# Where the first attention vectors of a four-layer graph network are folded: behind the first expert layer, or between the tiles of an edge count

## What is computed

```python
h = (x @ W.T).reshape(n, heads, out_ch)          # 8 heads of 128
a_src = jnp.einsum('nhc,hc->nh', h, att_src)
a_dst = jnp.einsum('nhc,hc->nh', h, att_dst)
e = leaky_relu(a_src[src] + a_dst[dst], 0.2)     # per edge, then softmax over dst
```

## Time and profile before

| what | value |
|---|---|
| median of 3 runs | 1740.7 us (1740.62 to 1742.16) |
| profiled execution, first to last instruction | 1740.0 us (the page gives no time of its own outside the span) |
| PE busy | 1682.7 us, 97% of the span |
| DVE, POOL, ACT busy | 931.1, 690.3, 466.8 us |
| mean granted TensorE clock | 0.988 |
| mean DMA rate | 57 GB/s |

### The profile page before, as it was taken

How to read it: one execution, slowest core, us unless ns; L and a number is a source line. 1 busy time by engine, 2 the same in 40 slices (tenths; PEclk the granted TensorE clock), 3 DMA queues, 4 the chain that set the end, 5 groups by cost and what they waited for, 6 DMA issues and landing times.

```text
span 1740.0 us, 25810 instructions
## 1 busy us (share of the span) xinstructions
PE 1682.7 (97%) x10227; PEld 1579.9 (91%) x10227; DVE 931.1 (54%) x1879; ACT 466.8 (27%) x875; POOL 690.3 (40%) x428
## 2 busy tenths in 40 slices
PE   8799999999999988899999999999999999999999
PEld 7699999997999988799377888989999999998999
DVE  8993537416866679857497554423112141225731
ACT  6443123203223138934222211101011011112310
POOL 1026865652445520060020175431644435342663
PEclk9899999999999999899899999999999999999999
DMA  2002222423212210014010022111221111110222
GB/s 90 1 28 70 73 69 65 142 78 128 64 55 64 64 56 10 1 47 143 7 43 1 11 85 64 57 45 37 73 64 55 46 51 59 55 55 30 64 73 72
DMA packets 42000, 99.84 MB, mean 57 GB/s; under 512 B 10509, under 2 KB 12143, under 8 KB 41895
## 3 DMA queue, kind: packets, MB, share of 16 engines
q1 hardware_dynamic: 37828, 87.87, 16.3%
q10 hardware_dynamic: 4066, 10.46, 1.7%
HBM read 96.39 MB, written 1.92 MB: 57 GB/s over the span
## 4 chain that ended last, share of the span: by engine, by line
PE 82%; DVE 11%; ACT 4%; issue 1%; POOL 1%; DVEq 0%; POOLq 0%; ACTq 0%
PE bank L2421 10%; PE bank L2423 10%; PE bank L2422 10%; PE banks L2421 9%; PE banks L2422 9%; PE banks L2423 9%; PE bank L2983 3%; PE banks L2983 3%; PE bank L3060 3%; PE bank L3065 3%; PE banks L3060 2%; PE banks L3065 2%; DVE tmp L1827 1%; DVE src_hot L1491 1%; PE banks L2835 1%
## 5 line engine op out<-in xcount | busy, mean ns | idle before, releaser
L833 POOL TENSOR_TENSOR w_hi<-raw,ones_r 128x768 fp32r<-128x768 f32 (+1 forms) x192 | 294.0, 1532 | 994.9 <-PE banks L2423 368.3
L836 POOL TENSOR_TENSOR w_lo<-raw,w_hi 128x768 fp32r<-128x768 f32 (+1 forms) x192 | 370.5, 1930 | 15.0
L2421 PE MATMUL bank<-w_hi,xT_hi 128*125 128x384 f32 (+2 forms) x560 | 187.8, 335 | 1.7 <-DVE small L1968 1.2
L2423 PE MATMUL bank<-w_hi,xT_lo 128*125 128x384 f32 (+2 forms) x560 | 186.7, 333 | 0.0
L2422 PE MATMUL bank<-w_lo,xT_hi 128*125 128x384 f32 (+2 forms) x560 | 186.5, 333 | 0.0
L2421 PE MATMUL banks<-w_hi,xT_hi 128*125 128x384 f32 (+2 forms) x440 | 151.8, 345 | 0.2 <-DVE xT_lo L1569 0.2
L2422 PE MATMUL banks<-w_lo,xT_hi 128*125 128x384 f32 (+2 forms) x440 | 151.4, 344 | 0.0
L2423 PE MATMUL banks<-w_hi,xT_lo 128*125 128x384 f32 (+2 forms) x440 | 151.3, 344 | 0.0
L1618 DVE TENSOR_TENSOR hT_lo<-tmp,hT_hi 128x312 fp32r<-128x312 f32 (+1 forms) x88 | 94.3, 1078 | 41.9 <-ACT hT_hi L970 41.5
L2421 PEld LDWEIGHTS bank<-w_hi,xT_hi 128*125 128x125 f32 x560 | 103.9, 186 | 5.0 <-DVE small L1968 1.4
L2422 PEld LDWEIGHTS bank<-w_lo,xT_hi 128*125 128x125 f32 x560 | 103.9, 185 | 2.5
(11 more groups left out here) (579 smaller groups left out, 3923.4 us busy)
## 6 DMA issues: line engine op xcount, KB each, us to landing
raw<-wa SPq DMA_DIRECT2D x92, 384.0 KB, 3.0
raw<-wc SPq DMA_DIRECT2D x76, 384.0 KB, 3.0
raw<-wb SPq DMA_DIRECT2D x28, 448.0 KB, 3.3
w_rows<-w_in ACTq DMA_DIRECT2D x1, 3072.0 KB, 12.6
bias<-bias_in ACTq DMA_DIRECT2D x6, 384.0 KB
w_first<-w_in ACTq DMA_DIRECT2D x1, 2304.0 KB, 11.2
w_down<-w_down_in SPq DMA_DIRECT2D x8, 288.0 KB, 5.2
w_up<-w_up_in SPq DMA_DIRECT2D x1, 2304.0 KB, 10.6
```

The source lines that it names most:

```text
L833: pool.tensor_tensor(w_hi[:, k, 0:width], raw[:, k, 0:width], ones[:, 0:1].to_broadcast([P, width]), ALU.mult).then_inc(S("unit_high"), 1)
L836: pool.tensor_tensor(w_lo[:, k, 0:width], raw[:, k, 0:width], f(w_hi[:, k, 0:width]), ALU.subtract).then_inc(S("unit_split"), 1)
L2421: tell_used(pe.matmul(dst, l_hi, r_hi, start=start, stop=False))
L2423: return pe.matmul(dst, l_lo, r_hi, start=False, stop=stop)
```

## The change

The fold moves to the front of the kernel, into span 1 of the edge count.

- **Transfers.** SP, not ACT, issues them, behind the first three units of weights. Seven heads go to `w1_first`, which lies where `w_hi` and `w_lo` will be, one to `w1_last`. POOL waits for the second `g2_fold` group before its first split.
- **PE.** `count_edges` gets a function `beside`. For span 1 the loop is written out, and behind each tile from 4 on `beside(t)` is called. Behind tile 6 it waits for the transfers; behind each of the tiles 6 to 21 it issues one of the 16 matmuls; behind tile 25 it issues the six transposes.
- **ACT.** Behind its `xn` tiles and ahead of the counts of span 1 it copies the two groups to `fold_T` and the turned ones to a new `fold_full`; behind the counts of span 1 it writes `folded_1` from that.
- **DVE.** The remainder is taken at the same place as before, from `fold_full`.
- **Banks.** The three groups get banks 2, 3 and 4 between spans 0 and 1, and the rotation ahead of f1 is put back to what it was.

```diff
-    def sweep(label, before_last=()):
+    def sweep(label, in_second=(), before_last=()):
         for i in range(SPANS * NT):
-            if i == LASTS:
-                for group in before_last:
-                    add(*group)
+            for group in in_second if i == NT else before_last if i == LASTS else ():
+                add(*group)
             add(label, i, label + "_settled", i + 1)
...
-    several("g2_fold", 2, "g2_fold_copied")
     several("g1a_agg", 2 * KD, "g1a_low")
-    several("g2_foldT", 1, "g2_fold_read")
...
             for k in range(RING):
                 sp.dma_start(raw[:, k, 0:UNIT], wa[k]).then_inc(S(f"raw_full{k}"), 16)
+            sp.dma_start(w1_first[:], w1_in[0:HEADS - 1].rearrange("h p k -> p h k")).then_inc(S("w1_loaded"), 16)
+            sp.dma_start(w1_last[:], w1_in[HEADS - 1]).then_inc(S("w1_loaded"), 16)
+            sp.dma_start(att_1[:], heads_in.rearrange("p h t e -> p h (t e)")).then_inc(S("w1_loaded"), 16)
...
+            await_group(pool, "g2_fold", 1)
             pool.wait_ge(*E("A_fraction", LASTS))
...
+            for c in range(2):
+                await_group(act, "g2_fold", c)
+                act.activation(fold_T[:, c * 384:(c + 1) * 384], bank("g2_fold", c)[0:16, 0:384], ACT.Copy
+                               ).then_inc(S("g2_fold_copied"), 1)
+            await_group(act, "g2_foldT", 0)
+            act.activation(fold_full[:], bank("g2_foldT", 0)[:, 0:16 * KD].rearrange("p (k c) -> p k c", c=16), ACT.Copy
+                           ).then_inc(S("g2_fold_taken"), 1)
             counts("A", adj, 1)
+            act.wait_ge(*E("g2_fold_taken", 1))
+            act.activation(folded_1[:, :, 0:16], fold_full[:], ACT.Copy).then_inc(S("g2_fold_high"), 1)
...
-            TT(folded_1[:, :, 32:48], bank("g2_foldT", 0)[:, 0:16 * KD].rearrange("p (k c) -> p k c", c=16),
-               f(folded_1[:, :, 0:16]), ALU.subtract).then_inc(S("g2_fold_read"), 1)
+            TT(folded_1[:, :, 32:48], fold_full[:], f(folded_1[:, :, 0:16]), ALU.subtract).then_inc(S("g2_fold_read"), 1)
...
                     for t in range(OSLOTS):
                         step(span, t, t, first=t == 0)
+                    if span == 1 and beside:
+                        for t in range(OSLOTS, tiles):
+                            step(span, t, t % OSLOTS, last_tile=t == tiles - 1)
+                            beside(t)
+                        continue
...
+            def fold_attention(t):
+
+                i = t - FOLD_FIRST
+                if i == 0:
+                    pe.wait_ge(*E("w1_loaded", 48))
+                if 0 <= i < 2 * HEADS:
+                    c, h = divmod(i, HEADS)
+                    dst = open_bank("g2_fold", c) if h == 0 else bank("g2_fold", c)
+                    weights = w1_first[:, h] if h < HEADS - 1 else w1_last[:]
+                    last = pe.matmul(dst[0:16, 0:384], att_1[:, h], weights[:, c * 384:(c + 1) * 384], start=h == 0,
+                                     stop=h == HEADS - 1)
+                    if h == HEADS - 1:
+                        close(last, "g2_fold", c)
+                if t == FOLD_TURN:
+                    pe.wait_ge(*E("g2_fold_copied", 2))
+                    pe.wait_ge(*E("consts", CONSTS))
+                    dst = open_bank("g2_foldT", 0)
+                    for k in range(KD):
+                        last = pe.transpose(dst[:, 16 * k:16 * k + 16], fold_T[:, k * P:(k + 1) * P], ident[0:16, 0:16])
+                    close(last, "g2_foldT", 0)
+
+            count_edges("A", greatest, fold_attention)
```

More of the change, by code:

```diff
@@ L86 @@
 ROWS_AT = {1: 0, 2: 1}
+FOLD_FIRST, FOLD_TURN = 6, 25
 SOURCES_AT = {3: (0, 1), 5: (2,), 7: (3,), 8: (4,), 10: (5,), 11: (6,), 13: (7,)}
@@ L273, in pairs @@
             add(label, i, label + "_read", i + 1)
-    sweep("A", (("g0_maxT", 0, "g0_max_read", 1), ("g0_maxB", 0, "g0_maxB_read", 1)))
+    sweep("A", (("g2_fold", 0, "g2_fold_copied", 1, False, 2), ("g2_fold", 1, "g2_fold_copied", 2, False, 3),
+                ("g2_foldT", 0, "g2_fold_taken", 1, False, 4)),
+          (("g0_maxT", 0, "g0_max_read", 1), ("g0_maxB", 0, "g0_maxB_read", 1)))
     spare = [1, 2, 7, 0, 3, 4, 5, 6]
@@ L296, in plan_groups @@
     turned_behind("g1b", "g1_x", "f1", between=lambda: several("g2_maskT", 2 * NT, "g2_masked"))
+    spare = spare[3:] + spare[:3]
     ffn("f1", 8)
@@ L454, in families @@
     base = 0
-    for event, n in (("g2_fold_copied", 2), ("g2_fold_high", 1), ("unit_rounded", 4), ("f2_column_exp", 1),
+    for event, n in (("g2_fold_copied", 2), ("g2_fold_taken", 1), ("g2_fold_high", 1), ("unit_rounded", 4), ("f2_column_exp", 1),
                      ("f2_row_exp", 1), ("f2_combine_high", 4), ("f2_activated", 1), ("f2_up_high", 4)):
@@ L572, in network @@
         folded_2 = at_("folded_2", [P, HEADS, 64], f32r, HT + 8 * NP * 4 + 7520)
-        w1_first = at_("w1_first", [P, 6, D], f32, XT + 15360)
+        fold_full = at_("fold_full", [P, KD, 16], f32, xt_lo_off + 15360 + KD * 64 * 4)
         w2_rows = at_("w2_rows", [P, HEADS, D], f32, HT + 15360)
@@ L585, in network @@
         raw = new("raw", [P, RING, UNIT_WIDE])
+        split_off = top[0]
         w_hi = new("w_hi", [P, RING, UNIT_WIDE], f32r)
         w_lo = new("w_lo", [P, RING, UNIT_WIDE], f32r)
+        w1_first = at_("w1_first", [P, HEADS - 1, D], f32, split_off)
+        assert split_off + (HEADS - 1) * D * 4 <= top[0]
         bias_off = region(D1 * 4)
@@ L660, in network @@
         uv = [at_(f"uv{i}", [TN, NT, 40], f32r, ht_lo_off + 8 * NP * 4 + 4096 + i * 800) for i in range(2)]
-        w1_last = at_("w1_last", [P, 2, D], f32, tmp_off)
-        att_1 = at_("att_1", [P, HEADS, 2 * HEADS], f32, tmp_off + 6144)
-        fold_T = at_("fold_T", [2 * HEADS, D], f32, HT + 52224)
+        w1_last = at_("w1_last", [P, D], f32, HT + 46080)
+        att_1 = at_("att_1", [P, HEADS, 2 * HEADS], f32, HT + 58496)
+        fold_T = at_("fold_T", [2 * HEADS, D], f32, NM + 24000)
         mean = at_("mean", [TN, 2, NT, HEAD_DIM], f32, tmp_off)
@@ L1102, in _ @@
             expert_layer("f0", 12, ACT.Gelu, True)
[L1104 to L1107, removed]
             normal_rows("g1")
@@ L1112, in _ @@
             act.dma_start(att_2[:], att_in.unsqueeze(0).to_broadcast([P, 2, D])).then_inc(S("w2_loaded"), 16)
[L1113 to L1116, removed]
             act.wait_ge(*E("g1_bias_used", 1))
@@ L1119, in _ @@
             messages_high("g1a", "g1a_agg", KD)
-            await_group(act, "g2_foldT", 0)
-            act.activation(folded_1[:, :, 0:16], bank("g2_foldT", 0)[:, 0:16 * KD].rearrange("p (k c) -> p k c", c=16),
-                           ACT.Copy).then_inc(S("g2_fold_high"), 1)
             for i in range(2 * NT):
@@ L2530, in of_rel, with count_edges @@
                 return lambda s, c0, cn: rel[:, r, s, c0:c0 + cn]
-            def count_edges(label, before_last=None):
+            def count_edges(label, before_last=None, beside=None):
                 def step(span, t, k, first=False, last_tile=False):
@@ L2643, in _ @@
             pe.wait_ge(*E("offset_row", 3))
-            count_edges("A", greatest)
+            def fold_attention(t):
[18 more added lines that the diff above has]
+            count_edges("A", greatest, fold_attention)
             def sum_edges(label, j, half, first, ready):
@@ L2690, in _ @@
             expert_layer("f0", 12, 0)
[L2692 to L2699, removed]
             pe.wait_ge(*E("self_loops", NT))
             gather("g1a_agg", KD, of_adj, "g1_nodes", lambda j, s: s + 1 if j == 0 else 0)
[L2703 to L2707, removed]
             down("g1a", "g1a", xT_hi, xT_lo, lambda k: pe.wait_ge(*E("g1a_low", 2 * k + 2)))
```

## The result

| what | before | after |
|---|---|---|
| median, runs side by side | 1740.73 us (4 runs, 1740.62 to 1742.16) | 1758.61 us (4 runs, 1757.08 to 1759.88) |
| ratio, 95% interval | | 1.0096, 1.0083 to 1.0109 |
| profiled execution, span | 1740.0 us | 1758.2 us |
| mean granted TensorE clock | 0.988 | 0.983 |

What follows compares the result with a forecast made beforehand. PE is 97% busy, but behind f0 the chain of waits runs through DVE and ACT; span 1 lacks PE room. +8.2 in span 1 and +1.1 behind f0 on 1740.0, plus 0.7, gave 1750.0 us, range 1745.5 to 1754.5.

Steps and rivals of the forecast that it cites:

- worth 0 on the path: Behind f0: removing the fold's 10.40 us of PE matmuls gains nothing, since the gather waits for DVE and ACT.
- rival 1: Behind f0: the gather waited for the fold, so moving it gives 1737.8 us; chance 7%.
- The pause and its price: At f0's end: PE stands some 8 of 12 us, its clock falls, and the gather's slow start costs +1.8 us.
- the 0.25 of waiting for `xT_lo`: Behind the gather, at 427.02: PE's wait for a bank DVE frees is absorbed if PE comes later, 0.25 us gained.
- Stage 1: What is taken from behind f0: -0.47 - 0.25 + 1.8 = +1.1 us, from -0.7 to +1.5.
- rival 4: Tile 6 of span 1: weights come late or push back other transfers, PE stands 11 us, 1761 us; chance 3%.
- rival 2: Span 1: PE's real room beside DVE takes in the whole fold, leaving 1741.8 us; chance 4%.
- The hand-over at the peak: Between spans 1 and 2: with PE later, DVE hands on 9.0 us of delay, not 10.35.
- The room in span 1: Span 1: PE waits 0.92 us for DVE, which added matmuls absorb.
- the change of kinds: Span 1: switching between bf16 and float32 matmuls 16 times, taken as 0, 1.4 us in the range, bound 6.9.
- Rival 3: Span 1: changing matmul kinds costs 0.43 us at each of 16 places, 6.9 more, 1756.9 us; chance 6%.
- 0.8 us back from the clock: Behind span 1: PE's shorter pause may keep its clock up, gaining 0 to 1.5 us; half taken, 0.8.

Runs made afterwards that it cites:

- the first experiment: The kernel before with 14 of the fold's 16 float32 matmuls left out at their old place: 1746.3 us, ratio 1.0019.
- the bf16 run: The kernel before with six more bf16 matmuls behind each of tiles 6 to 22 of span 1, fold in its old place: 1753.45 us, ratio 1.0056.
- The kernel with the early rotation: The kernel after with the bank rotation put around the gather of graph layer 1 instead of ahead of f1: 1758.91 us, ratio 1.009.
- the second experiment: The kernel after with 14 of the 16 fold matmuls left out, transfers, copies, transposes and banks kept: 1744.32 us, ratio 1.0011.

## Why the forecast was right and wrong

**Right: the old place.** That the matmuls there are "worth 0 on the path" is shown by the first experiment, and against rival 1 (the fold was what the gather waited for): 9.1 us less there gained nothing. The pause and its price were there too. PE waited 10.2 us where about 8 were forecast, the gather's first matmuls ran at half clock, and the stages fell back by 15.85 - 14.40 = 1.45 us (14.40 is 421.65 less the 407.25 of the earlier trace rows, 15.85 the difference at 410 us) where 1.8 had been put. Of that, 15.85 - 14.67 = 1.2 came back by 430 us: the six transposes (0.47), the 0.25 of waiting for `xT_lo`, and 0.5 that the forecast didn't have and that the first experiment, with its transposes in place, gets back too. Stage 1 cost +0.2 instead of +1.1, within its bounds. The first experiment paid 1.4 there.

**Right: the direction and the absorbed parts of span 1.** PE was the later one, DVE waited for it, the weights came in time (rival 4 falls), and span 1 had no room for the fold (rival 2 falls). The hand-over at the peak gave back 14.02 - 12.66 = 1.36 us where 1.35 was forecast; that the two agree is partly luck, since without the transposes, in the bf16 run, it gave back 0.74. The room in span 1 was 1.1 us there, against 0.92.

**Wrong, and the largest: the change of kinds.** The step that failed is "I take 0, since the one start of a new kind in the earlier trace rows (49.28 behind 49.19) costs 0.09", with 1.4 in the range. That row shows a float32 matmul behind bf16 ones with nothing behind it but a pause: one piece of three. Coming back costs 0.10 + 0.05 more. With 0.24 at the 16 matmuls and 0.14 at the transposes (0.09 in, 0.05 out) the sum for the span is 10.4 + 0.47 + 4.0 - 1.1 (19.77 - 28 x 0.667, PE's waits for DVE) = 13.8, measured 13.81, where 10.35 stood (its 0.4 for waits ahead of the matmuls was not there). Rival 3 had the mechanism at 0.43 us each and 6.9 in all; the measured prices make 4.0. At 6% it was held too unlikely: no row excluded it, and the 0 was the bound and not an estimate.

**Wrong: 0.8 us back from the clock.** The half-clock stretch behind span 1 came in after as in before, 3.4 us each (67.1 against 53.0 in the earlier trace rows). The shorter pause did not keep the clock up; through span 2 and the sums the stages lose 0.6 (12.66 to 13.28) instead.

**Overlooked: the rotation of the banks** ahead of f1, listed in the change and costed nowhere: 0.65 us at 520, in both profiles of after and in the two experiments that keep it, and gone in the one that moves it.

**Left open: 2.7 us in the medians, 4.6 in the profiles.** The terms shown are 12.7 in front, 0.2 at f0's end and 0.65 at f1, 13.6 in all, against 16.3 (12.0 to 18.5 by the interval of the second set) in the medians and 18.2 in the profiles. What is left in the profiles is 0.6 up to 120 us, 1.15 at 130 (the stretch at 138.8, where the matmuls behind the degrees step by 0.26 us instead of 0.145), 2.65 at 650 (the one at 664.5) and 0.2 behind it. The two large ones are half-clock stretches that fall on full work in some traces and not in others. The kernel with the early rotation lacks the first of them, and has still the same median. The second may belong to the old place: taking matmuls away there cost 3.3 us in the medians, and only 1.4 of it lies at f0's end in the trace. Then "worth 0" is right for the matmuls and too good for what their absence does to the clock later on. That is argued from where the stretches fall, and no run shows it by itself: the second experiment has the same pause and the same stretch, and its median is only 1.3 us above before's.

## What to carry to other kernels

Read the price of a moved piece at both places from the chain of waits, and not from the busy share: at 97% busy, 9 us of matmuls were worth nothing behind f0, 10.4 us were free in the gaps of span 2, and the same 10.4 cost all of themselves and their joints in span 1. Where a piece is cut up to fit between other work, price the joints, there and back, with rows that show both directions; here no row did, and the middle of the bounds, 3.4 us, would have been nearer to the measured 4.0 than the lower end was. And for a difference of less than half a per cent take the spread of the kernel before from more than three runs, and compare stages before totals.

## What the hardware did that was not expected

A bf16 matmul sequence interrupted by one of the fold's float32 matmuls loses 0.24 us beyond the matmul's own 0.65 (0.09 on the way in, 0.10 and 0.05 on the way out); over a whole span, one run instead of sixteen saved 0.205 a piece, or 0.23 without a wait for DVE.

The same passage of the same work has a half-clock stretch behind it in one trace and none in another: behind 1.51 of 3.40 us busy, after has one at 664.5 and before has none. And not every stretch stands behind a pause of PE: from 135.40 to 138.80 after's PE is recorded as busy for 3.40 of 3.40 us, with a row of 25 matmuls of only two columns from 136.41 on, and the clock is 0.50 from 138.8 on, in both of its profiles. In before the same work has no stretch behind it. Together the stretches moved stages of one and the same program between two executions by +1.5 us (at 100) to -2.1 (at the end), more than several of the terms that were argued over.
